# Diffusion steps on one core: tile 0's Sobel and first two steps moved forward, tile 1's coefficients behind them

## The chip, the cores and the metric

The kernel runs on 1 core of a Trainium2 chip: TensorE (PE), VectorE (DVE), ScalarE (ACT), GpSimd (POOL) and SyncE (SP) with a shared SBUF, PSUM in four slots of 1024 columns for this kernel, and 16 DMA engines. The time is the device time of one execution in microseconds; the median of 3 runs is compared.

## The reference, cut to what matters

The input is x of 8 x 32 x 32 x 64. A group norm gives s. A depthwise 3x3 convolution gives g and g1, Sobel gives the diffusivities, and five explicit steps of an advection and diffusion scheme follow. Its result is added to x, and a second part adds a ternary 3x3 convolution.

```python
gy, gx = _sobel(h)
Dx = 1.0 / (gy * gy / LAM2 + 1.0)
Dy = 1.0 / (gx * gx / LAM2 + 1.0)
ux = 0.5 * (jnp.roll(g, 1, axis=2) - jnp.roll(g, -1, axis=2))
vy = 0.5 * (jnp.roll(g1, 1, axis=3) - jnp.roll(g1, -1, axis=3))
Ax, Ay = (g * DT, g1 * DT)
Bx, By = (Dx * DT, Dy * DT)
E = (ux + vy) * DT
D = 1.0 / (1.0 + 2.0 * Bx + 2.0 * By)
cm_x, cp_x = (-Ax + 2.0 * Bx, Ax + 2.0 * Bx)
cm_y, cp_y = (-Ay + 2.0 * By, Ay + 2.0 * By)
c0 = 1.0 - 2.0 * Bx - 2.0 * By
for _ in range(K):
    prev = h
    h = D * (c0 * h0 - 2.0 * E * h + cm_x * jnp.roll(h, 1, axis=2) + cp_x * jnp.roll(h, -1, axis=2)
             + cm_y * jnp.roll(h, 1, axis=3) + cp_y * jnp.roll(h, -1, axis=3))
    h = h + D * (2.0 * DT) * fsrc
    h0 = prev
...
x = x + _L0_conv_ref(_gn(x), ...)   # the part above, with its last norm and relu
x = x + _L1_conv_ref(_gn(x), ...)   # y = conv(x, alpha * ternary(W)), relu(y + b)
```

## The kernel before

The batch is cut into two tiles of four images. A tile lies in SBUF with 128 partitions (image row and image) and planes of 2048 float32 columns (W x C); "a plane" below is one such 128 x 2048 block. `coef` holds seven planes of coefficients for each tile: AXP, AXM, AYP, AYM and AE multiply the four neighbours and the centre in a step, A0 the state before the last, and FS is the source. `ring` has three planes; early on they hold x, squares, regrouped s (`s_grouped`), g1 of tile 0 and `e0`, later the products.

The program is written per engine, in one fixed order, with semaphores between the engines. No scheduler moves anything. PSUM slots are given out by the table `early` in `job_table` and by the rows that the function adds from ORDER; TensorE takes a slot for a job (`take`) once the reader of the last job there has signalled (`wait_reader`).

The head of a tile, in its order: sums over the groups (`sum_x`, `centre`, `square_of`, `sum_squares`), small matmuls `mean_t` and `var_t`, rsqrt by Ln and Exp on ScalarE. Then `scale_grouped` (line 718) writes scaled s in another order of columns for the turns `t2`, and `scale_s` scales s in place. `split_hi` and `split_lo` cut s into two parts of reduced float32 for Sobel, which TensorE runs in passes over the high and the low part (`sobel`, line 1095): gy and gx, two halves each. ScalarE squares them into coef planes 0 and 1. `depthwise` (line 1123) makes g and g1 (PSUM jobs `cv_t_q`), which ScalarE reads with `to_natural`. VectorE's `shifted`, `denominator`, `newton`, `across_rows`, `across_columns`, `both_diffusivities` turn the squares into the coefficients, with one inverse by ScalarE's Ln and Exp (`reciprocal_first`), and `over_rows` and `over_channels` finish AXM, AXP, AYM and AYP of a tile.

GpSimd's queue carries DMAs that add one SBUF plane to another. For tile 0 the divergence e is made from VectorE's `channel_difference` (three instructions, the last signals `e_made`) and two pairs of adding DMAs (`e_some`, `e_full`), and `divergence_added` (line 873) turns it into AE. For tile 1 TensorE makes it (`divergence`, line 1145, two halves of two banks). Other adding DMAs are `other_rows` (AXM, semaphore `ax_full`), `other_channels` (AYM, `ay_full`), `first_source` (the plane `first_two` that TensorE adds in steps 0 and 1, `first_full`), the sum of tile 1's two diffusivities (`sb_added`, behind a copy by SP, `sb_begun`) and the kept plane of each later step.

A step (k, t) is `step` on VectorE (line 978): five products of a coefficient and the shifted state into the ring, and for k from 1 to 3 a sixth plane, the A0 product kept for the next step. TensorE adds each product into PSUM by 16 transposing matmuls (`add_products`), as well as the source or the kept plane (`add_source`), and turns the result back to natural order (`back_to_natural`) after ScalarE has copied it out (`keep_turned`, `keep_state`, `wrap` for the halo). VectorE can be at most three products ahead of TensorE. The steps of both tiles alternate by ORDER:

```python
ORDER = [(0, 0), (1, 0), (0, 1), (2, 0), (1, 1), (3, 0), (2, 1), (4, 0), (3, 1), (4, 1)]
```

Behind the steps stand the residual, the second group norm (`spread`, `second_norm`, `normalise`), the dense convolution as `dense` with high and low parts, and the way back (`out_natural`).

## Time and profile before

| | us |
|---|---|
| median of 3 runs (278.44 to 280.2) | 278.44 |
| the profiled execution, its own time | 277.91 |
| its span, first to last instruction | 276.1 |
| VectorE busy | 247.2 (90%) |
| TensorE busy | 233.6 (85%) |
| ScalarE busy | 133.8 (48%) |

The profile is of one execution. A line of the order of time gives the start, the time from the first start to the last end of the group, the engine, the line of the kernel, what it writes and reads, how many instructions there are, and in brackets the idle time of the engine ahead of it with what ended it. ScalarE's calls all carry line 380, a helper's, and VectorE's fused ones line 653; they are told apart by their tiles and times. Matmul ends are modelled; the distance between starts is the better measure.

### The profile page before, as it was taken

How to read it: one execution, taken by the hardware profiler on the slowest of the kernel's cores; microseconds unless marked ns; L12 is line 12 of the kernel's file. 1: busy time of each engine (PE TensorE's matmuls, PEld its weight loads, DVE VectorE, ACT ScalarE, POOL GpSimd, SP SyncE). 2: the span in 40 equal slices, each digit the busy share in tenths (PEclk: the TensorE clock that was granted, in tenths of full speed). 3: DMA queues.
4: the chain of work that ended last, by engine and by line, in shares of the span. 5: the costliest groups of instructions: out<-in, count | busy, mean ns of one | idle time of the engine just before them, and what ended most of it. 6: DMA issues, size and time to landing. Idle time of an engine off the chain costs nothing.

```text
span 276.1 us, 5235 instructions
## 1 busy us (share of the span) xinstructions
PE 233.6 (85%) x2276; PEld 209.6 (76%) x2276; DVE 247.2 (90%) x196; ACT 133.8 (48%) x207; POOL 16.8 (6%) x36
## 2 busy tenths in 40 slices
PE   0137999999959999279999999999999987889793
PEld 0136889989925588279989999898989986767683
DVE  3799999999999989999998999999999989886821
ACT  3294776879860054702623425160603246917743
POOL 2000000003310201101000101010101000000000
PEclk9999999999979999959999999999999999999999
DMA  6950000005998771990700334248610030000124
GB/s 213 350 116 0 0 4 6 2 0 112 199 205 253 152 152 38 209 209 2 154 0 2 76 78 94 61 116 190 129 26 1 0 138 17 2 0 0 62 93 152
DMA packets 7190, 24.94 MB, mean 90 GB/s; under 512 B 2816, under 2 KB 3328, under 8 KB 5120
## 3 DMA queue, kind: packets, MB, share of 16 engines
q0 software_dynamic: 2304, 14.68, 26.6%
q1 hardware_dynamic: 4720, 9.61, 10.6%
q10 hardware_dynamic: 144, 0.33, 0.4%
q8 instruction: 18, 0.29, 0.4%
q14 instruction: 4, 0.03, 0.0%
HBM read 6.79 MB, written 2.10 MB: 32 GB/s over the span
## 4 chain that ended last, share of the span: by engine, by line
DVE 54%; PE 27%; issue 9%; ACT 7%; DMA 1%; DVEq 0%; ACTq 0%
DVE ring L918 24%; DVE coef L653 8%; PE psum L1180 8%; PE psum L1170 6%; ACT coef L380 5%; PE psum L1257 5%; DVE first_two L1004 4%; PE psum L1117 3%; PE psum L1087 3%; DVE state L729 2%; DVE coef L964 1%; DMA bn<-in_norms 1%; DVE ring L722 1%; DVE hi_s L734 1%; DVE gsum L687 1%
## 5 line engine op out<-in xcount | busy, mean ns | idle before, releaser
L918 DVE TENSOR_TENSOR ring<-coef,state 128x2048 f32<-128x2048 f32 x51 | 113.5, 2286 | 2.1 <-PE psum L1180 1.9
L1180 PE MATMUL psum<-mats,ring 128*128 128x128 f32 x816 | 96.6, 278 | 9.6 <-DVE ring L918 9.5
L1180 PEld LDWEIGHTS psum<-mats,ring 128*128 128x128 f32 x816 | 91.4, 144 | 13.3 <-DVE ring L918 12.9
L380 ACT ACTIVATE state<-psum 128x1024 f32<-128x1024 f32 x36 | 35.1, 1028 | 74.3 <-PE psum L1180 60.2
L653 DVE SCALAR_TENSOR_TENSOR coef<-coef 128x2048 f32<-128x2048 f32 x16 | 36.4, 2290 | 0.7 <-issue 0.2
L380 ACT ACTIVATE coef<-coef 128x2048 f32<-128x2048 f32 (+1 forms) x10 | 17.6, 1783 | 10.1 <-DMA coef<-coef 9.9
L1257 PE MATMUL psum<-hi,dense_m 128*128 128x512 f32 (+1 forms) x54 | 20.0, 379 | 0.9 <-ACT coef L380 0.9
L1139 PEld LDWEIGHTS psum<-coef,state 32*128 32x128 f32 x672 | 19.4, 187 | 1.4 <-issue 1.3
L380 ACT ACTIVATE coef<-psum 128x512 f32<-128x512 f32 (+2 forms) x23 | 17.5, 766 | 5.4 <-PE psum L1117 4.3
L1139 PE MATMUL psum<-coef,state 32*128 32x64 f32 x672 | 20.0, 271 | 0.0
L1257 PE MATMUL psum<-lo,dense_m 128*128 128x512 f32 (+1 forms) x54 | 19.5, 369 | 0.0
L1180 PE MATMUL psum<-mats,first_two 128*128 128x128 f32 x144 | 17.3, 273 | 1.8 <-issue 1.2
L1180 PEld LDWEIGHTS psum<-mats,first_two 128*128 128x128 f32 x144 | 15.9, 141 | 2.3 <-ACT state L380 1.4
L1087 PE MATMUL psum<-mats,state 128*128 128x128 f32 x128 | 15.4, 273 | 0.7 <-ACT state L380 0.7
L1087 PEld LDWEIGHTS psum<-mats,state 128*128 128x128 f32 x128 | 14.1, 141 | 1.2 <-ACT state L380 1.1
L380 ACT ACTIVATE coef<-coef,gn 64x512 f32<-64x512 f32 x9 | 11.3, 1322 | 3.4 <-DVE gn L653 3.4
L975 DVE TENSOR_TENSOR coef<-coef 128x512 f32<-128x512 f32 (+2 forms) x7 | 5.4, 767 | 8.2 <-ACT coef L380 8.1
L1117 PE MATMUL psum<-hi_s,sobel_m 128*128 128x512 f32 (+2 forms) x48 | 12.1, 391 | 0.2 <-DVE hi_s L734 0.2
L1170 PE MATMUL psum<-coef,mats 128*128 128x512 f32 (+2 forms) x20 | 9.6, 616 | 3.1 <-ACT first_two L380 3.1
L1257 PEld LDWEIGHTS psum<-hi,dense_m 128*128 128x128 f32 x54 | 10.2, 188 | 2.7 <-issue 1.1
L380 ACT ACTIVATE coef<-psum,outp,wred 128x512 f32<-128x512 f32 (+2 forms) x7 | 5.9, 838 | 13.0 <-PE psum L1257 13.0
L1270 PE MATMUL psum<-gsum,mats 128*128 128x32 f32 x4 | 1.2, 404 | 12.2 <-DVE gsum L687 12.2
(133 smaller groups left out, 280.4 us busy)
## 6 DMA issues: line engine op xcount, KB each, us to landing
first_two<-coef POOLq DMA_DIRECT2D x7, 1024.0 KB, 8.5
coef<-coef POOLq DMA_DIRECT2D x5, 1024.0 KB, 8.8
coef<-in_x SPq DMA_DIRECT2D x2, 1024.0 KB, 6.0
coef<-in_wide_taps SPq DMA_DIRECT2D x3, 384.0 KB, 7.6
ring<-in_x SPq DMA_DIRECT2D x2, 512.0 KB, 6.0
ring<-in_x SPq DMA_DIRECT2D x1, 1024.0 KB, 10.3
coef<-coef SPq DMA_DIRECT2D x1, 1024.0 KB, 7.6
out<-coef SPq DMA_DIRECT2D x2, 512.0 KB, 3.1
```

The lines of the kernel that those rows point to most:

```text
L380: return nc.scalar.activation(dst, src, func, **kw)
L653: return V.scalar_tensor_tensor(out=out_ap, in0=in0, scalar=scalar, in1=in1, op0=op0, op1=op1)
L729: signal(V.tensor_tensor(s, s, root(t).unsqueeze(1).broadcast_to([128, W, C]), ALU.mult), s_ready, t + 1)
L918: V.tensor_tensor(wc(ring[:, slot, :]), wc(coef[:, t, a, :]), h_at(t, k, dw, dc), ALU.mult)\
L975: V.tensor_tensor(part(coef[:, t, 3, :], t, h), part(coef[:, t, 0, :], t, h), part(coef[:, t, 2, :], t, h), ALU.add).then_inc(sum_ready, 1)
L1004: V.tensor_tensor(wc(first_two[t][:, :]), wc(coef[:, t, A0, :]), h_at(t, k), ALU.mult)\
L1087: ins = nc.tensor.transpose(dst[:, j * 128:j * 128 + 128], src, ident)
L1117: ins = mm(dst[:, bank * BANK + to * C:bank * BANK + (to + count) * C], sobel_m[:, m, :], part[:, frm * C:(frm + count) * C], start=(i == ...
L1139: ins = mm(banks[a][:, j * 2 * W:(j + 1) * 2 * W], sT[t][p, 8 * h + j, dy * BT:dy * BT + 128], taps(8 * h + j)[p, dy, :, :].rearrange("p v ...
L1170: ins = mm(out_ap, m, src, start=(i == 0), stop=(i == len(pieces) - 1), skip_group_check=True)
L1180: ins = mm(slot_ap(name)[:, (j % 8) * 128:(j % 8) * 128 + 128], src[:, j * 128:j * 128 + 128], ident, is_transpose=True, start=first and j ...
L1257: ins = mm(to, dense_m[:, b, dy, :], rows[:, j0 + b:j1 + b, dy * BT:dy * BT + 128], start=(n == 0), stop=(n == len(steps) - 1))
```

## The change

The kernel does the same arithmetic with other orders and other homes for some work.

- VectorE scales s first and reorders it by a plain copy (`reorder`). Tile 0's high part and tile 1's reorder go to ScalarE.
- TensorE runs 12, 5 and 8 matmuls on `sobel_m` whose results nobody reads (`keep_warm`) between the small ones. Sobel of tile 0 comes ahead of its turns `t2`, gy's two high passes ahead of its low ones; tile 1's Sobel comes behind tile 1's depthwise and has SBUF of its own for its two parts.
- The divergence of tile 1 moves on TensorE from ahead of all steps to two places: a half after step (0, 0), a half after step (1, 0).
- VectorE runs tile 0's source and step (0, 0) ahead of tile 1's newton, with AE, `denominator(1)` and a small request between the products, and step (1, 0) ahead of tile 1's `over_rows`.
- GpSimd's queue runs both pairs of e first, then AXM, AYM and first_two of tile 0, then the rest.
- ScalarE's order for tile 1 follows. The last rsqrt stands ahead of `relu_dense(0, 0)`.
- `both_diffusivities`, `d_of(0)` and the first of `over_rows(0)` run in halves. The ring is used in falling order.

```diff
 (VectorE)
-            scale_grouped(0)
+            scale_s(0)
+            reorder(0)
             mean_of(1)
...
             threshold()
-            scale_s(0)
-            split_hi(0)
             split_lo(0)
             centre(1)
             sum_squares(1)
...
-            ternary()
+            ternary_count()
             ask_scale(1)
-            ternary_sign()
+            ternary_kept()
             rsqrt(128, GROUPS, root(1), wide=True)
-            scale_grouped(1)
+            scale_s(1)
             shifted(0)
             denominator(0)
-            scale_s(1)
+            weight_scale()
+            ternary_sign()
             split_hi(1)
             split_lo(1)
             newton(0)
             across_columns(0)
+            channel_difference()
             across_rows(0)
             both_diffusivities(0)
-            channel_difference()
             over_rows(0)
...
-            denominator(1)
             over_channels(0)
+            source(0)
+            step(0, 0, ((1, divergence_added), (2, lambda: denominator(1)), (3, ask_out)))
             newton(1)
+            out_norm()
             across_rows(1)
             across_columns(1)
-            divergence_added()
...
-            step(0, 0)
+            step(1, 0)
             over_rows(1)
             over_channels(1)
             divergence_taken()
             source(1)
-            step(1, 0)
 (VectorE's reorder)
+                dve.wait_ge(s_ready, t + 1)
+                V.tensor_copy(s_grouped[t].rearrange("p (g a w e) -> p a w g e", e=2, a=CP, w=W),
+                              h_at(t, 0).rearrange("p w (a g e) -> p a w g e", a=CP, e=2)).then_inc(s_grouped_ready, 1)
 (GpSimd)
-            other_rows(0)
             pool.wait_ge(e_some, 32)
             pool.wait_ge(minus_ready, 1)
             pool.dma_start(e0[:, 0:N - C], minus_g[:, C:N], accum_op=ALU.add).then_inc(e_full, 16)
             pool.dma_start(e0[:, N - C:N], minus_g[:, 0:C], accum_op=ALU.add).then_inc(e_full, 16)
+            pool.wait_ge(e_full, 32)
+            other_rows(0)
             other_channels(0)
+            first_source(0)
             pool.wait_ge(sb_begun, 16)
 (TensorE)
+            def keep_warm(name, count):
+
+                to = take(name)[:, 0:BANK]
+                pe.wait_ge(sobel_m_ready, 4)
+                for _ in range(count):
+                    mm(to, sobel_m[:, 0, :], sobel_m[:, :, :].rearrange("p m n -> p (m n)"), start=True, stop=True)
+
             group_mean(0)
+            keep_warm("gx_0_0", 12)
             group_var(0)
+            keep_warm("gx_0_0", 5)
             group_mean(1)
...
             small("wsum", 1, ones[:, :], wred[:, 0:1])
-            to_depthwise(0, 0)
-            to_depthwise(0, 1)
-            pe.wait_ge(sobel_m_ready, 4)
-            sobel(0, 0, 0)
-            sobel(0, 0, 1)
+            keep_warm("gx_0_0", 8)
+            for n in range(2):
+                sobel(0, 0, 0, (n,))
+                sobel(0, 0, 1, (n,))
...
-            divergence(0)
-            divergence(1)
+            for g in range(2):
+                for h in range(2):
+                    sobel(1, g, h)
             last = None
             for k, t in ORDER:
-                if last is None:
-                    take_sums(t, k)
-                    add_products(t, k, ((2, lambda: add_source(*reversed(ORDER[0]), False)),), True)
-                    last = (k, t)
-                    continue
-                if last[0] < STEPS - 1 and last[1] == t:
+                if last is not None and last[0] < STEPS - 1 and last[1] == t:
+                    back_to_natural(*last)
+                if (k, t) == ORDER[1]:
+                    divergence(0)
+                if (k, t) == ORDER[2]:
+                    divergence(1)
                     back_to_natural(*last)
                 if (k, t) == ORDER[-1]:
                     group_mean2(0)
                 take_sums(t, k)
+                if k == 0:
+                    add_products(t, k, ((3, lambda: add_source(t, 0, False)),), True)
+                    last = (k, t)
+                    continue
                 add_source(t, k)
 (ScalarE, the last norm)
             relu_bn_out(1, 0)
             relu_bn_out(1, 1)
+            rsqrt_first(128, BT)
             relu_dense(0, 0)
-            rsqrt_first(128, BT)
             normalise(1)
```

On GpSimd's queue, behind the first pair of e, the program before has this order (`coef<-coef` at line 316 is AXM, 321 is AYM, 340 the sum of tile 1's diffusivities, 335 and 336 the second pair of e):

```order
L330 DMA ring<-coef 128x1984 [waits e_made]
L331 DMA ring<-coef 128x64
L316 DMA coef<-coef 128x2048 [waits axp_ready]
L335 DMA ring<-state 128x1984 [waits minus_ready,e_some]
L336 DMA ring<-state 128x64
L321 DMA coef<-coef 128x2048 [waits ayp_ready]
L340 DMA coef<-coef 128x2048 [waits column_part,sb_begun]
L327 DMA first_two0<-coef 128x2048 [waits s_copied0,source_ready]
```

The changed program has the same queue in this order (326 is AXM, 331 AYM, 352 the sum, 344 and 345 the second pair):

```order
L340 DMA ring<-coef0 128x1984 [waits e_made]
L341 DMA ring<-coef0 128x64
L344 DMA ring<-state 128x1984 [waits minus_ready,e_some]
L345 DMA ring<-state 128x64
L326 DMA coef0<-coef0 128x2048 [waits axp_ready,e_full]
L331 DMA coef0<-coef0 128x2048 [waits ayp_ready]
L337 DMA first_two0<-state 128x2048 [waits s_copied0,source_ready]
L352 DMA coef1<-coef1 128x2048 [waits column_part,sb_begun]
```

AXM moved behind the end of e, and tile 0's first_two moved in front of tile 1's sum.

On VectorE, the changed program has this around step (0, 0); `ring<-coef0,state` is a product, 917 is AE, the lines 683 on coef1 are `denominator(1)` and `newton(1)`:

```order
L683 SCALAR_TENSOR_TENSOR state<-coef0,state 128x2048 [waits pe_job]
L960 TENSOR_TENSOR ring<-coef0,state 128x2048 [waits pe_job,axp_ready,ayp_ready,s_halo]
L960 TENSOR_TENSOR ring<-coef0,state 128x2048 [waits dense_m_ready]
L917 TENSOR_TENSOR coef0<-ring,coef0 128x2048 [waits e_full,d_ready,axp_ready]
L960 TENSOR_TENSOR ring<-coef0,state 128x2048 [waits ae_ready]
L683 SCALAR_TENSOR_TENSOR coef1<-coef1 128x2048 [waits shifted_ready,slot_free1,slot_free0]
L960 TENSOR_TENSOR ring<-coef0,state 128x2048 [waits ring_free,ax_full0,u_ready]
L1060 TENSOR_SCALAR rs_in<-outp 128x1 [waits outp_in]
L960 TENSOR_TENSOR ring<-coef0,state 128x2048 [waits ring_free,ay_full0,rs_asked]
L683 SCALAR_TENSOR_TENSOR coef1<-coef1 128x2048 [waits y_ready]
```

Before, all of `denominator(1)`, `newton(1)`, the two across planes and AE stood ahead of the first product; now the first two products stand ahead of AE and the rest of tile 1 stands between or behind.

On TensorE, the changed program has this from the fourth product of step (0, 0) on (1229 adds a plane by 16 transposes, 1134 turns back, 1219 is the divergence):

```order
L1229 MATMUL psum<-mats,ring 128x128 x15
L1229 MATMUL psum<-mats,first_two0 128x128 [waits first_full0]
L1229 MATMUL psum<-mats,first_two0 128x128 x15
L1229 MATMUL psum<-mats,ring 128x128 [waits product]
L1229 MATMUL psum<-mats,ring 128x128 x15
L1134 MATMUL psum<-mats,state 128x128 [waits slot_free0]
L1134 MATMUL psum<-mats,state 128x128 x7
L1134 MATMUL psum<-mats,state 128x128 [waits slot_free1]
L1134 MATMUL psum<-mats,state 128x128 x7
L1219 MATMUL psum<-coef1,mats 128x512 [waits slot_free2,slot_free3,slot_free1,slot_free0]
```

Before, the source came behind the third product, and both halves of the divergence ahead of the first.

## Rows read from the trace of the kernel before

**Rows 1.** The page, part 1: busy time, share of the span, instructions.

```profile
PE 233.6 (85%) x2276; PEld 209.6 (76%) x2276; DVE 247.2 (90%) x196; ACT 133.8 (48%) x207; POOL 16.8 (6%) x36
```

**Rows 2.** VectorE's order of time, head; columns as told under the profile.

```profile
19.87 2.29 DVE L722 TENSOR_TENSOR ring<-state,gsum 128x2048 f32<-128x2048 f32 x1
...
24.75 1.23 DVE L734 CAST hi_s<-state 128x2048 fp32r<-128x2048 f32 x1
...
35.55 0.19 DVE L714 TENSOR_SCALAR rs_in<-psum 128x32 f32<-128x32 f32 x1 [0.37 <-PE psum L1276]
```

**Rows 3.** ScalarE's order of time: copy_s(0), d_of(1) with a0_of(1), wrap of state 1.

```profile
78.77 1.97 ACT L380 ACTIVATE first_two<-state 128x2048 f32<-128x2048 f32 x1
...
97.51 3.73 ACT L380 ACTIVATE coef<-coef 128x2048 f32<-128x2048 f32 x2 [9.93 <-DMA coef<-coef]
...
111.45 0.71 ACT L380 ACTIVATE state<-state 128x64 f32<-128x64 f32 x4
```

**Rows 4.** VectorE's order of time, from the end of channel_difference to step (2, 0).

```profile
63.36 0.21 DVE L871 TENSOR_TENSOR ring<-ring 128x32 f32<-128x32 f32 x1
...
98.49 4.49 DVE L918 TENSOR_TENSOR ring<-coef,state 128x2048 f32<-128x2048 f32 x2 [1.16 <-PE psum L1180]
102.90 4.61 DVE L653 SCALAR_TENSOR_TENSOR coef<-coef 128x2048 f32<-128x2048 f32 x2
...
129.84 11.10 DVE L918 TENSOR_TENSOR ring<-coef,state 128x2048 f32<-128x2048 f32 x5
...
148.23 4.50 DVE L918 TENSOR_TENSOR ring<-coef,state 128x2048 f32<-128x2048 f32 x2 [0.69 <-PE psum L1180]
```

**Rows 5.** TensorE's order of time: first Sobel passes, and tile 1's turns behind tile 0's depthwise.

```profile
26.12 2.50 PE L1117 MATMUL psum<-hi_s,sobel_m 128*128 128x512 f32 x7 [0.22 <-DVE hi_s L734]
28.45 1.65 PE L1117 MATMUL psum<-lo_s,sobel_m 128*128 128x512 f32 x7
...
50.43 2.19 PE L1087 MATMUL psum<-mats,ring 128*128 128x128 f32 x16
```

**Rows 6.** TensorE's order of time: divergence, step (0, 0) and step (2, 0).

```profile
84.76 1.96 PE L1170 MATMUL psum<-coef,mats 128*128 128x512 f32 x4
...
96.44 5.44 PE L1180 MATMUL psum<-mats,ring 128*128 128x128 f32 x48
102.52 1.97 PE L1180 MATMUL psum<-mats,first_two 128*128 128x128 f32 x16 [0.65 <-DMA first_two<-coef]
104.32 3.66 PE L1180 MATMUL psum<-mats,ring 128*128 128x128 f32 x32
108.32 1.98 PE L1087 MATMUL psum<-mats,state 128*128 128x128 f32 x16 [0.34 <-ACT state L380]
...
146.28 8.90 PE L1180 MATMUL psum<-mats,ring 128*128 128x128 f32 x80
```

**Rows 7.** GpSimd's and SP's order of time: DMA issues around e and tile 1's sum.

```profile
72.02 0.86 POOL L335 DMA_DIRECT2D ring<-state  x1 [2.51 <-DMA ring<-coef]
...
90.53 0.86 POOL L340 DMA_DIRECT2D coef<-coef  x1 [13.66 <-DMA coef<-coef]
...
82.67 0.51 SPq L289 DMA_DIRECT2D coef<-coef  x1
```

**Rows 8.** Stretches: us, TensorE busy, its granted clock, DMA share, GB/s.

```profile
79.20:84.70 5.50, 5.50 (x14) 0.71 1.06 205
...
92.00:97.00 5.00, 5.00 (x23) 1.00 0.99 198
...
118.00:121.00 3.00, 2.04 (x10) 0.50 1.09 216
```

**Rows 9.** The page, part 6: adding DMAs between planes of coef, median us to landing.

```profile
coef<-coef POOLq DMA_DIRECT2D x5, 1024.0 KB, 8.8
```

**Rows 10.** ScalarE's and VectorE's order of time: relu ahead of the last rsqrt.

```profile
249.70 1.21 ACT L380 ACTIVATE coef<-psum,outp,wred 128x1024 f32<-128x1024 f32 x1 [7.01 <-PE psum L1257]
...
251.27 0.16 DVE L670 TENSOR_TENSOR rs_t<-rs_y 128x4 f32<-128x4 f32 x1 [1.91 <-ACT rs_y L380]
```

285 lines of the change are left out of this document (159 added, 126 removed), and 6 rows, old and new, of the table early.

## Prediction

> **What bounds the kernel now.** The page's busy line [rows 1] shows VectorE busy for 247.2 of 276.1 us and TensorE for 233.6. VectorE's order of time [rows 2, 4] shows that it hardly waits between the first mean and 98 us. Each step of the recurrence then costs it six full planes at 2.2 us, 13.2 us; TensorE needs seven passes of 16 transposes at 1.75 us, 12.3 us (80 took 8.90 in [rows 6]). So TensorE has 0.9 us to spare in a step, and only after a step without a sixth plane (k = 0) does it make VectorE wait: 1.16 us at 98.49 and 0.69 us at 148.23 [rows 4]. I read the change at two places: where VectorE ends tile 0's first step together with tile 1's inverse (102.98 before), and where it makes the fourth product of step (2, 0) (148.23 before). From there to the last norm both programs are alike and VectorE does not wait.
>
> All times are on the axis of the profiled execution: its span is 276.1 us, its own time 277.91 us, and the median of the three runs 278.44. I sum changes of the span and take them from 278.44.
>
> **The head, up to e.** On VectorE the change removes two scale_grouped at 2.29 and one cast at 1.23, and adds one reorder of a full plane [rows 2]. The trace has no such copy; its bounds are the cast (1.23) and the strided scale_grouped (2.29). I take 1.23, the price of a one-source full plane here. Removed: 4.6 us (3.5 with the other bound). Waits come in return:
> - s is ready at 19.87 + 2.29 = 22.2. ScalarE's high part is a full plane out of state, 1.97 as in copy_s [rows 3]: 24.2, where the cast ended at 25.98. VectorE is there at 23.8 and waits 0.4.
> - The warm-up matmuls stand between the sums: 12 of 512 columns from about 11.6. Seven at the slow start took 2.50 us [rows 5], 0.36 each, twice the full rate would be 0.43, so 12 end at 15.9 to 16.8; var_0's sums are ready at 16.65. Cost 0 to 0.15, taken as 0. If they work, the first Sobel pass takes 1.65 and not 2.50.
> - TensorE: four passes of 1.5 us from 24.3, then gx_0_0 (2.1), then var_1 at 32.5. VectorE waits 0.4 for it, as it does now (0.37 in [rows 2]). Sobel ends at 35.1, the turns of tile 0 at 37.0, and after ScalarE's copy and alpha the depthwise of tile 0 runs from 37.3, 13.1 us. It ends at 50.4, as before [rows 5]: this side gains nothing.
> - ScalarE: squares to 36.1, two copies to 38.1, four taps to 39.2, reorder(1) as a full plane to 41.2, Ln and Exp of tile 0 to 45.2. VectorE is through denominator, alpha, sign and tile 1's parts at 46.2: hidden by 1.0. Were reorder(1) 2 us slower, 1 us would show.
> - channel_difference now stands ahead of across_rows and needs cv_0_3 read. ScalarE reads cv_0_2 from 50.5 (1.0), then copies half of t2_1 (1.0), then reads cv_0_3 (1.0): 53.6. VectorE is there at 53.1 and waits 0.5.
>
> So e is made at 56.2 instead of 63.57 [rows 4]; across_rows, the two halves of both_diffusivities, the first over_rows (in halves as well, behind d_of's halves of 1.0), over_channels and source, seven planes of 2.3, end at 72.4.
>
> **Tile 0's first step.** Two products (76.8), AE (79.1), its product (81.3), denominator(1) (83.7; shifted(1) is done at 79.1, since TensorE's Sobel of tile 1 runs from 65.8 to 75.9), product (85.9), product (88.3). Newton(1) needs ScalarE's Ln and Exp of the denominator: 87.7, hidden. With newton 4.6, the output norm 1.2 and two across planes 4.6 VectorE is at 98.7. Before, the same list ended at 102.98: gain 4.3, of which 1.16 is the old wait at 98.49, and 4.6 removed less 0.9 of new waits and some halves make the rest.
>
> **The adding DMAs, which become the bound.** The queue works in order and moves 198 GB/s while it adds [rows 8], so 1 MB takes 5.3 us after 1.5 us of start: the one issued at 90.53 was waited for until 97.51, the next until 102.52 [rows 3, 6, 7]. From e made to the second pair went 63.57 to 72.02, 8.45 us [rows 4, 7]. So the first pair runs 56.2 to 64.65, and the second, now alone on the queue, 0.8 + 7.0 more: 72.5. Then three adds follow together, 1.5 + 3 x 5.3: AXM 79.4, AYM 84.8, first_two0 90.1. AXM and AYM are needed at 83.7 and 86.1: hidden by 4.3 and 1.3. first_two0 is not: TensorE has added the fourth product by 87.8 and must add the source before the fifth. Its order is then source 91.9, fifth product 93.7, turns back to natural 96.0 (2.3 later, as 107.98 to 110.30 in [rows 6]), half the divergence at 3.9 per bank (three banks from 84.76 to 96.44): 103.8. Then source of (1, 0) 105.6, first product 107.3. The halo of state 1 comes 4.2 after the fifth product (107.98 to 112.16 in [rows 3, 6]): 97.9, just hidden by VectorE's 98.7.
>
> VectorE makes three products of (1, 0) by 105.3 and then finds the ring full until 107.4: a new wait of 2.1. Two products and the kept plane: 114.0. Tile 1's d is ready at 96.4 + 7.9 (SP's copy, 82.67 to 90.53 in [rows 7]) + 7.0 (add) + 2.1 = 113.4, hidden by 0.6. Tile 1's rows, channels, divergence and source are six planes, 13.8: step (0, 1) starts at 127.8, before at 129.84. Gain left 2.0.
>
> **Step (0, 1).** Its source moves from the front to place 3, in front of the fifth product. TensorE ends the fourth at 138.5 and the fifth at 142.0; then source and turns of (2, 0) and one product, 5.3 more: VectorE's fourth product of (2, 0) starts 19.6 after the step's start, before 18.4 (129.84 to 148.23). Minus 1.2. Further, TensorE has nothing from 125.5 to 130.1. After such a gap the granted clock was 0.50 (the 1.2 GHz level) in 118 to 121 [rows 8], so its first passes run slow: 0 to 1.0, I take 0.6. So 148.23 becomes 148.0: **gain 0.2 of the 4.3**.
>
> **The tail.** The last rsqrt moves in front of relu_dense(0, 0). ScalarE stood idle when it was asked, but ran 1.21 us of relu first; VectorE waited 1.91 [rows 10]. VectorE is free 1.5 earlier, ScalarE's three pieces 1.05, TensorE's dense(1, 0), which follows the low half, 1.3. From there it is TensorE's work to the end: **minus 1.3**.
>
> Sum: 0.2 + 1.3 = 1.5, 278.44 - 1.5 = **276.9 us**.
>
> **A rule weighed.** From 92 to 97 us the adds moved 198 GB/s [rows 8]. The Trainium skill, DMA: Bandwidth & Descriptors, section Measured (HBM→SBUF), gives 6.15 us and 341 GB/s for one transfer of 1 MB issued from GpSimd. By that rate three adds would take an estimated 9.2 us of transfer instead of 16, first_two0 would be there near 83, and the sum would be that of rival 2. That table is for plain loads, and this trace disagrees with it for adds within SBUF.
>
> **The rivals.**
> 1. The clock falls in tile 0's first step. TensorE works there in pieces, with gaps of 2.0, 2.7 and 2.2 us from 79 to 90. For: after an idle stretch of 3 us it averaged 0.71 in 79.2 to 84.7 [rows 8]. Against: shorter gaps left it at 1.00. A slow pass costs 1.75 more, and one to two are on the path of first_two0: 1.7 to 3.5, 279.3. It decides over the sum from any fall at 90.
> 2. VectorE stays the bound: e or the adds are earlier and first_two0 lands before 88, so the 2.1 wait goes, and with it the 0.6: 274.2. For: the 1.5 of start is read from one pair only. Against: 198 GB/s.
> 3. Slower: the adds don't overlap their fixed parts, and each lands 8.8 us after the last (the median of five in [rows 9]). first_two0 lands at 98.9, 8.8 later, and all to 148 with it: 285.7. It makes the kernel slower by 1% once first_two0 lands after 94.5. Against it: the pair at 90.53.
> 4. The warm-up does nothing: the first high pass stays 0.85 longer, and var_1 with it: 277.7. Against it: TensorE runs at full rate from 28.45 [rows 5], after some 6 us of work, and would have had that work before.
>
> **How the numbers follow.** The likeliest, the sum as worked out, 0.45 (its own range 275.0 to 278.8: reorder 0 to 1.1, slow start 0 to 1.0, one microsecond either way for the head); rival 1 0.19; rival 2 0.22; rival 3 0.06; rival 4 0.08. Range 273.8 to 280.0, from rival 2 to the middle of rival 1. One percent, 2.8 us, is about what a measurement of this kernel can tell. Faster by more: rival 2 and a fifth of the likeliest, 0.31. Slower by more (over 281.2): rival 3 and the upper end of rival 1, 0.11. The rest 0.58.
>
> **What would show it.** The high part on ScalarE ends near 24.2; e is made near 56; three adds are issued together at 72 to 73; TensorE waits for the DMA of first_two0 until 90, with the clock beside it; VectorE waits some 2 us for TensorE in the fourth product of (1, 0), and again in that of (2, 0); step (0, 1) starts near 127.8; the wait for the last rsqrt is 0.4 instead of 1.91. The prediction is wrong if VectorE doesn't wait in (1, 0), if first_two0 lands away from 90, or if ScalarE's strided reorder costs far more than 2 us.

## Result: 0.7% slower

| | changed kernel | kernel before |
|---|---|---|
| median of 20 runs each | 280.76 us (278.16 to 283.38) | 278.56 us (277.73 to 280.2) |
| ratio, 95% interval | 1.0069 (1.0052 to 1.0086) | 1 |
| profiled execution: own time, span | 283.38, 281.6 us | 277.91, 276.1 us |
| VectorE, TensorE busy | 243.5, 242.6 us | 247.2, 233.6 us |
| mean granted clock of TensorE | 0.964 | 0.981 |

The forecast was 276.9 us, with a range to 280.0. The profiled execution of the changed kernel is the longest of its twenty, 2.6 us over the median, and one of three slow ones that the ratio leaves out; its late times exceed those of a median run by up to as much. Experiments are compared by their ratios, and a difference between two of them carries the intervals of both. The page, part 1, of the changed kernel (it answers [rows 1]):

```profile
PE 242.6 (86%) x2301; PEld 216.9 (77%) x2301; DVE 243.5 (86%) x196; ACT 138.2 (49%) x210; POOL 16.9 (6%) x36
```

VectorE does 3.7 us less, as the change intends, and the kernel is still slower. The time went into waits. VectorE's order of time, changed kernel, those waits (it answers [rows 2, 4]):

```profile
34.62 0.19 DVE L744 TENSOR_SCALAR rs_in<-psum 128x32 f32<-128x32 f32 x1 [2.05 <-PE psum L1325]
...
55.84 2.23 DVE L908 TENSOR_TENSOR ring<-ring 128x1984 f32<-128x1984 f32 x1 [1.18 <-ACT ring L391]
...
85.20 2.29 DVE L683 SCALAR_TENSOR_TENSOR coef<-coef 128x2048 f32<-128x2048 f32 x1 [1.84 <-ACT coef L391]
...
103.98 6.70 DVE L960 TENSOR_TENSOR ring<-coef,state 128x2048 f32<-128x2048 f32 x3 [1.55 <-ACT state L391]
113.39 2.29 DVE L960 TENSOR_TENSOR ring<-coef,state 128x2048 f32<-128x2048 f32 x1 [2.71 <-PE psum L1229]
...
133.71 8.89 DVE L960 TENSOR_TENSOR ring<-coef,state 128x2048 f32<-128x2048 f32 x4
...
154.92 4.50 DVE L960 TENSOR_TENSOR ring<-coef,state 128x2048 f32<-128x2048 f32 x2 [2.94 <-PE psum L1229]
```

In order: var_1 from TensorE 2.05 (0.37 before); channel_difference 1.18; tile 1's shifted magnitudes at denominator(1) 1.84; the halo of state 1 1.55; the full ring in (1, 0) 2.71; the fourth product of (2, 0) 2.94 (0.69 before, at 148.23). TensorE's order of time, changed kernel, shows what they wait for (it answers [rows 5, 6]):

```profile
20.12 2.08 PE L1332 MATMUL psum<-sobel_m 128*128 128x512 f32 x8
24.38 4.50 PE L1165 MATMUL psum<-hi_s,sobel_m 128*128 128x512 f32 x14 [2.17 <-ACT hi_s L391]
...
62.66 4.01 PE L1188 MATMUL psum<-coef,state 32*128 32x64 f32 x133
68.38 0.55 PE L1188 MATMUL psum<-coef,state 32*128 32x64 f32 x10 [1.71 <-issue]
...
94.64 3.38 PE L1229 MATMUL psum<-mats,first_two 128*128 128x128 f32 x16 [1.89 <-DMA first_two<-state]
...
136.14 10.01 PE L1229 MATMUL psum<-mats,ring 128*128 128x128 f32 x64 [6.28 <-DVE ring L960]
```

Each stall is followed by slow work. Stretches of the changed kernel (length, TensorE busy, then its weight loads and the other engines; the granted clock is third from the right, then DMA share and GB/s):

```profile
26.00:28.00 2.00, 2.00 (x6) 1.62 (x5) 2.00 (x3) 1.10 (x5) 0.00 (x0) 0.50 0.00 0
...
70.00:72.00 2.00, 2.00 (x16) 1.70 (x13) 2.00 (x1) 1.78 (x4) 0.00 (x0) 0.57 1.28 254
...
92.00:94.00 2.00, 0.75 (x4) 0.35 (x2) 2.00 (x2) 0.00 (x0) 0.00 (x0) 0.50 0.37 74
...
136.00:142.00 6.00, 5.86 (x28) 5.89 (x29) 6.00 (x3) 0.00 (x0) 0.00 (x0) 0.50 0.98 198
```

0.50 is the 1.2 GHz level. The pause of 1.71 us at 66.67 has no releaser in the trace ("issue") and no counterpart before.

### The profile page after: what moved, and what is told of

It is laid out like the page before. It is cut to its first block, busy times and chain, and to the rows that moved or that the text cites. A ratio compares the mean times of both kernels' runs of the same rounds, so it can differ in the third digit from the quotient of the medians.

```text
span 281.6 us, 5289 instructions
## 1 busy us (share of the span) xinstructions
PE 242.6 (86%) x2301; PEld 216.9 (77%) x2301; DVE 243.5 (86%) x196; ACT 138.2 (49%) x210; POOL 16.9 (6%) x36
## 4 chain that ended last, share of the span: by engine, by line
DVE 28%; PE 20%; issue 3%; ACT 1%; DVEq 0%; ACTq 0%
DVE ring L960 19%; PE psum L1229 12%; PE psum L1306 4%; DVE first_two L1046 3%; PE psum L1134 3%; DVE coef L1006 2%; DVE coef L968 1%; DVE stats L973 1%; DVE coef L1017 1%; DVE lo L1012 0%; DVE coef L925 0%; ACT state L391 0%; ACT coef L391 0%; DVE gn L683 0%; PE psum L1285 0%
## 5 line engine op out<-in xcount | busy, mean ns | idle before, releaser
L1229 PE MATMUL psum<-mats,ring 128*128 128x128 f32 x816 | 98.2, 280 | 12.7 <-DVE ring L960 12.6
L1229 PEld LDWEIGHTS psum<-mats,ring 128*128 128x128 f32 x816 | 92.8, 145 | 16.1 <-DVE ring L960 9.2
L683 DVE SCALAR_TENSOR_TENSOR coef<-coef 128x2048 f32<-128x2048 f32 (+1 forms) x17 | 36.6, 2164 | 2.3 <-ACT coef L391 1.8
L391 ACT ACTIVATE coef<-coef 128x2048 f32<-128x2048 f32 (+2 forms) x10 | 16.0, 1614 | 10.2 <-DMA coef<-coef 7.1
L1229 PE MATMUL psum<-mats,first_two 128*128 128x128 f32 x144 | 18.7, 287 | 1.9 <-DMA first_two<-state 1.9
L1229 PEld LDWEIGHTS psum<-mats,first_two 128*128 128x128 f32 x144 | 17.4, 150 | 2.3 <-DMA first_two<-state 2.3
L1165 PE MATMUL psum<-hi_s,sobel_m 128*128 128x512 f32 (+2 forms) x48 | 13.9, 438 | 2.2 <-ACT hi_s L391 2.2
L1165 PEld LDWEIGHTS psum<-hi_s,sobel_m 128*128 128x128 f32 x48 | 10.2, 227 | 4.5 <-issue 2.6
L1306 PEld LDWEIGHTS psum<-hi,dense_m 128*128 128x128 f32 x54 | 10.1, 188 | 3.0 <-issue 1.1
L1165 PE MATMUL psum<-lo_s,sobel_m 128*128 128x512 f32 (+2 forms) x48 | 11.6, 383 | 0.0
L1046 DVE TENSOR_TENSOR first_two<-coef,state 128x2048 f32<-128x2048 f32 x5 | 11.4, 2289 | 0.0
```

The costliest lines, as they stand in the source:

```text
L391: return nc.scalar.activation(dst, src, func, **kw)
L683: return V.scalar_tensor_tensor(out=out_ap, in0=in0, scalar=scalar, in1=in1, op0=op0, op1=op1)
L1046: V.tensor_tensor(wc(first_two[t][:, :]), wc(coef[t][:, A0, :]), h_at(t, k), ALU.mult)\
L1165: ins = mm(dst[:, bank * BANK + to * C:bank * BANK + (to + count) * C], sobel_m[:, m, :], part[:, frm * C:(frm + count) * C], start=(i == ...
L1229: ins = mm(slot_ap(name)[:, (j % 8) * 128:(j % 8) * 128 + 128], src[:, j * 128:j * 128 + 128], ident, is_transpose=True, start=first and j ...
L1306: ins = mm(to, dense_m[:, b, dy, :], rows[:, j0 + b:j1 + b, dy * BT:dy * BT + 128], start=(n == 0), stop=(n == len(steps) - 1))
```

## Experiments

Each ratio is to the kernel before. "Unread matmuls" are matmuls whose result nobody reads. Three theories compete. **Clock**: TensorE's granted clock falls after each gap. **Chain of adds**: tile 0's source lands too late. **Sobel(1) late**: tile 1's Sobel now stands behind depthwise(1), and VectorE needs it in the middle of step (0, 0).

**tail_only**: the kernel before, with the last rsqrt ahead of relu_dense(0, 0).

```diff
-            relu_dense(0, 0)
             rsqrt_first(128, BT)
+            relu_dense(0, 0)
             normalise(1)
```

> The kernel before with one edit of the change: the last rsqrt ahead of relu_dense(0, 0). All theories expect VectorE's wait there to fall from 1.91 to 0.4 us and the end to come 1.2 to 1.3 us earlier: 277.3 us, ratio 0.9955. If it stays at 1.00 the tail's gain is lost again in the dense part.

277.38 us, 0.9962 (0.9946 to 0.9978): 1.06 us gained of 1.3 forecast. VectorE's wait of 1.91 [rows 10] became 0.38. So the other parts of the change together cost 1.07 points, some 3.0 us.

**fill_gaps**: the changed kernel with unread matmuls in TensorE's gaps.

```diff
-            keep_warm("gx_0_0", 8)
+            keep_warm("gx_0_0", 18)
...
+                    keep_warm("acc_0_1_0", 22)
...
+                    if (k, t) == ORDER[0]:
+                        between = ((2, lambda: keep_warm("dv_1_0", 8)), (3, lambda: keep_warm("dv_1_0", 9))) + between
```

> The changed kernel with matmuls nobody reads in three gaps of TensorE: 18 instead of 8 ahead of Sobel, 8 and 9 behind the third and fourth product of step (0, 0), 22 ahead of step (0, 1). The clock theory (slow passes after gaps: 24.4, 70, 91 and 136 us in the profile of the changed kernel) expects 2 to 4 us back: 277 to 279 us, and a narrower spread of runs, since the fall depends on the run. The theory of the adding DMAs (first_two0 is what binds, the slow passes are mostly hidden) expects at most 1 us: 280 us.

281.41 us (280.96 to 281.93), 1.011 (1.0093 to 1.0128). The mean clock rose from 0.964 to 0.986 and e was made 2.0 us earlier (56.3), yet the kernel is 1.1 us slower than the changed one. VectorE's wait at denominator(1) grew to 3.52. The clock alone is not the cause. In step (2, 0) TensorE waited 1.62 us for the kept plane's add, a wait that I had not seen coming.

**div_gap**: divergence(0) between the third and the fourth product of (0, 0), into TensorE's gap of 2.6 us.

```diff
-        if i == 1:
+        if i == 0:
             jobs.append(("dv_1_0", 2))
...
-                if (k, t) == ORDER[1]:
-                    divergence(0)
...
+                    if (k, t) == ORDER[0]:
+                        between = ((2, lambda: divergence(0)),) + between
```

> The changed kernel with the first half of tile 1's divergence moved on TensorE from behind step (0, 0) to between its third and fourth product, where TensorE has nothing to do. The theory that the divergence stands on the path of VectorE's ring expects the wait of 2.71 us in step (1, 0) to vanish, and the slow source pass with it: 3 to 4 us, 277 to 278 us. If the adds alone bind, the halo of state 1 stays where it is and only the ring wait goes: 278 us. The clock theory without the path expects 1 us: 279.7.

280.61 us, 1.0085 (1.0054 to 1.0116): no gain. The full ring's wait of 2.71 us is gone, but the halo's wait rose to 2.07 and the one at denominator(1) was 3.44.

**no_ewait**: GpSimd no longer waits for the second pair before it issues tile 0's adds.

```diff
-            pool.wait_ge(e_full, 32)
             other_rows(0)
```

> The changed kernel without GpSimd's wait for e between the second pair and AXM (the add of AXM touches nothing of e). The theory that the chain of adds binds expects AXM's transfer to start right behind e's, 3 to 4.5 us earlier, first_two0 as much earlier, and 2 to 3 us off the time: 278 us. Against it: AXM's transfer may hold up the end of e's pair, then AE is late and the time stays at 280.5. The clock theory alone expects at most 1 us.

279.92 us, 1.0045 (1.002 to 1.007): 0.7 us under the changed kernel, which is less than the two intervals together. AXM, AYM and the source are issued at 67.5, 72.0 and 74.2 instead of 76.2 to 77.3, and TensorE no longer waits for the source; VectorE waits 3.44 at denominator(1) instead. Whether the adds are part of it is open until queue_both.

**den_late**: denominator(1) behind the fifth product.

```diff
+            rsqrt_first(128, 1)
             reciprocal_first(1)
-            rsqrt_first(128, 1)
...
-            step(0, 0, ((1, divergence_added), (2, lambda: denominator(1)), (3, ask_out)))
-            newton(1)
+            step(0, 0, ((1, divergence_added), (3, ask_out), (4, lambda: denominator(1))))
             out_norm()
+            newton(1)
```

> The changed kernel with denominator(1) behind the fifth product of step (0,0), so that VectorE no longer waits in the middle of that step for the shifted magnitudes of tile 1. Theory 'Sobel(1) is late' (wait of 1.84 us in the profile of the changed kernel, 3.44 us in two variants of it): the five products of step (0,0) end 1.5 to 3.4 us earlier, and of that 1 to 2 us reach the end, 278.5 to 280 us; newton(1) may then wait for ScalarE's Ln and Exp. Theory 'TensorE's clock': the wait is only moved, and the time stays at 280.5 to 281.5 us. Theory 'the chain of adds': the ready adds still land at their time, so the halo wait in front of step (1,0) grows by what was gained, 280 to 281 us.

282.45 us, 1.0129 (1.0095 to 1.0162): slower than the changed kernel by 1.7 us. VectorE's order of time, den_late, and the issue of AYM's add at 76.25 with its time to landing:

```profile
83.33 2.29 DVE L960 TENSOR_TENSOR ring<-coef,state 128x2048 f32<-128x2048 f32 x1 [0.52 <-PE psum L1229]
...
89.27 2.29 DVE L960 TENSOR_TENSOR ring<-coef,state 128x2048 f32<-128x2048 f32 x1 [3.58 <-issue]
...
97.85 9.22 DVE L683 SCALAR_TENSOR_TENSOR coef<-coef 128x2048 f32<-128x2048 f32 x4 [2.92 <-ACT coef L391]
```

```profile
coef<-coef POOLq DMA_DIRECT2D x1, 1024.0 KB, 12.9
```

With denominator(1) out of the way the fourth product waits 0.52 us itself, for TensorE: it starts to add products only when Sobel(1) ends, at 81.3, and the ring has three planes. The fifth waits 3.58, and not for TensorE: it needs AYM, whose add was issued at 76.25 and landed 12.9 us later, at 89.2, and the product starts at 89.27. In the changed kernel AYM landed at 89.70 and the fifth product started at 89.91: it was hidden by 0.2 us, behind the wait at denominator(1). So two bounds lie close together here, Sobel(1) and the adds. newton(1) then waits 2.92 us for ScalarE's inverse, which now starts later, and step (1, 0) begins at 107.0 and not at 104.0.

**sobel_fill**: 18 instead of 8 unread matmuls ahead of Sobel(0), the first line of fill_gaps alone.

> The changed kernel with 18 instead of 8 unread matmuls between Sobel(0)'s coefficients being asked for and its first pass; nothing else. Theory 'TensorE's clock': the 14 high-pass matmuls of Sobel(0) take 3.0 instead of 4.5 us, VectorE's wait for var_1 (2.05 us) falls under 0.5, the gain of tile 0 is made by 56.3 instead of 58.3, and the time falls by 1.5 to 2 us to about 279 us. Theory 'what comes behind': the earlier gain is eaten by waits for Sobel(1) and the adds, and the time is within 0.7 us of the changed kernel's.

279.51 us, 1.0038 (1.0015 to 1.0062): 0.9 us gained on the changed kernel. The wait for var_1 fell to 0.44, the first pair was issued 1.6 us earlier, and the wait at denominator(1) grew to 4.31. TensorE's order of time and stretches, sobel_fill:

```profile
66.53 1.33 PE L1188 MATMUL psum<-coef,state 32*128 32x64 f32 x19 [1.69 <-issue]
```

```profile
66.00:68.00 2.00, 1.47 (x28) 1.47 (x32) 2.00 (x2) 1.93 (x7) 1.46 (x2) 0.50 0.12 24
68.00:70.00 2.00, 2.00 (x46) 2.00 (x43) 1.97 (x2) 0.04 (x1) 0.29 (x1) 0.50 1.18 230
70.00:72.00 2.00, 2.00 (x14) 1.65 (x14) 1.93 (x2) 1.55 (x4) 0.00 (x0) 0.50 0.93 190
72.00:74.00 2.00, 2.00 (x7) 1.61 (x6) 2.00 (x2) 0.52 (x2) 0.00 (x0) 0.50 0.55 87
```

The pause is there again, ten matmuls earlier in depthwise(1, 1) with ten more in front of it: behind the 850th matmul since the start, as in the changed kernel. Behind it the clock is at 0.50 until 74. That eats the gain: Sobel(1) ends at 82.9, in the changed kernel at 81.8.

**kept_first**: GpSimd's add of (2, 0)'s kept plane ahead of tile 1's whole-tile adds.

```diff
+            keep(1, 0)
             other_rows(1)
...
-            for k, t in ORDER:
+            for k, t in ORDER[2:]:
```

> The changed kernel with GpSimd's add of the kept plane for step (2,0) put ahead of tile 1's whole-tile adds. Theory 'the kept plane is late' : step (2,0)'s fourth product no longer waits 2.9 us for TensorE, and up to 1.3 us comes off, 279.5 us. Theory 'TensorE's clock' : the stall of TensorE ahead of step (0,1) stays, (2,0) stays as late, and the time is within 0.5 us of the changed kernel's. The add now stands ahead of tile 1's adds in the queue and could hold them for 5.3 us: then step (0,1) starts later and the time rises by 1 to 3 us.

280.2 us, 1.0049 (1.0025 to 1.0073), 0.2 points under the changed kernel, less than the two intervals together. VectorE's wait in (2, 0) was 2.10.

**no_warm**: the three keep_warm counts at 0.

> The changed kernel without its 25 unread matmuls (counts 12, 5 and 8 set to nothing). Theory 'TensorE's clock': the box sums and Sobel(0) run at the lower clock, var_0 and var_1 come 1 to 3 us later, the gain of tile 0 is made at 60 to 61 and the time rises by 2 to 3 us to about 283 us. Theory 'the warm-up warms nothing that matters': within 0.7 us of the changed kernel. TensorE's unexplained pause of 1.7 us in depthwise(1,1) stays at its place among the instructions if it is tied to the program, and goes if it is tied to what TensorE did before.

283.96 us, 1.0184 (1.0159 to 1.0209): the warm-up is worth 3.2 us, a little over the 2 to 3 that I expected. The pause shrank to 0.93 us. It stands later in depthwise(1, 1) but again behind some 850 matmuls, since 25 are missing in front.

**sobel_early**: TensorE's Sobel(1) and ScalarE's squares ahead of depthwise(1), with the PSUM slots to match; of the edit TensorE's part:

```diff
...
-            depthwise(1, 0)
-            depthwise(1, 1)
             for g in range(2):
                 for h in range(2):
                     sobel(1, g, h)
+            depthwise(1, 0)
+            depthwise(1, 1)
```

> The changed kernel with TensorE's Sobel of tile 1 ahead of the depthwise sums of tile 1, as the kernel before had it; ScalarE's squares go with it, and nothing else changes. Theory 'the order depthwise, then Sobel, is the harm': TensorE's pause of 1.7 us in the depthwise sums of tile 1 and the half clock behind it no longer stand ahead of the shifted magnitudes, VectorE's wait at denominator(1) goes (1.84 to 4.3 us so far), and the products of step (0,0) end 2 to 3 us earlier. What reaches the end is bounded by the adds, since the source of tile 0 is needed ahead of the fifth product and lands near 94 us as before: 1 us, 279.5 to 280. Theory 'TensorE has the same work to do and is the bound from 24 to 88 us': the wait only moves to the products, and the time is within 0.5 us of the changed kernel's.

285.98 us, 1.0257 (1.0227 to 1.0286), a miss that both theories share: source(0) writes the buffer out of which depthwise(1) reads, and VectorE waited 9.37 us for it. The change's order of the two is forced by that buffer. The pause was there all the same (1.11 us, the clock at 0.50 in 77 to 79), again behind the 848th matmul, although these now include all 48 of Sobel(1). So it belongs to a count of TensorE's instructions and not to Sobel's place.

**best2** is no_ewait, sobel_fill and kept_first together; **best3** adds sobel_early to it, **best4** div_gap to best3.

> The three single edits without sobel_early: no wait for the second e pair ahead of tile 0's adds, 18 unread matmuls ahead of Sobel(0), the kept plane's add ahead of tile 1's. Alone they were worth 0.8, 0.9 and 0.5 us. Theory 'each cures its own delay': 278.3 to 278.8 us. Theory 'the wait for the shifted magnitudes of tile 1 is what they all run into': it grows to 4 us or more and the time stays at 279.3 to 280 us; the difference to best3 is then what the order of Sobel and depthwise costs.

> sobel_early together with the three single edits that gained: no wait for the second e pair ahead of tile 0's adds, 18 instead of 8 unread matmuls ahead of Sobel(0), and the kept plane's add ahead of tile 1's. If the parts add up, 0.9 + 0.8 + 0.5 and what sobel_early is worth: 277.5 to 278.5 us, even with the kernel before or just ahead of it. If one bound takes over from the next, as the wait for shifted(1) did when the others were taken away, 279 to 280 us.

> best3 with the first half of tile 1's divergence between the third and fourth product of step (0,0), where TensorE waits for VectorE. With the source of tile 0 landed in time, the half divergence (3.9 us) is off the path from the fifth product to the first sum of step (1,0), and the full ring in (1,0) (1.6 us in the profile without the wait for the e pair) goes: up to 1.5 us under best3 if that wait is the bound there; within 0.5 us of best3 if VectorE only waits later, in step (2,0).

best2: 278.95 us, 1.0014 (0.9993 to 1.0034), level with the kernel before; the parts nearly add up (0.24 + 0.31 + 0.20 points expected, 0.55 measured). best3: 286.14 us, 1.0234; best4: 286.74 us, 1.0283; both carry sobel_early's wait and tell no more. In best2 TensorE still waits 6.28 us ahead of (0, 1), then takes 9.93 us for 64 transposes, and the pause is there.

**no_e_adds**: the changed kernel without the four adding DMAs into e and the waits for them. This leaves out two of e's terms; it measures only what they cost.

```diff
-            pool.dma_start(e0[:, C:N], gN[0][:, 0:N - C], accum_op=ALU.add).then_inc(e_some, 16)
...
-            pool.dma_start(e0[:, N - C:N], minus_g[:, 0:C], accum_op=ALU.add).then_inc(e_full, 16)
```

> The changed kernel without the two pairs of adding DMAs into e and without the waits for them; this leaves out part of the computation of e, and its time is only for comparison. The adds of tile 0 are then issued from 67.5 us, and the queue is empty while TensorE runs the first part of the depthwise sums of tile 1. Theory 'the adds' transfers hold up TensorE's load of instructions': the pause of 1.7 us in the depthwise sums of tile 1 goes, the clock stays at 1.00 from 66 to 76, Sobel(1) ends near 79 instead of 81.8, and VectorE's wait at denominator(1) is 0 to 1.5 us instead of 1.84 to 3.4. Theory 'the pause belongs to the program': it stays at its place with 1.5 to 1.8 us. In both cases the source of tile 0 lands by 88 us, so TensorE doesn't wait for it: with the pause gone 277.5 to 278.5 us, with it 279 to 279.8.

276.43 us, 0.992 (0.9896 to 0.9944): 4.1 us under the changed kernel. TensorE's order of time and two stretches, no_e_adds:

```profile
63.02 4.25 PE L1179 MATMUL psum<-coef,state 32*128 32x64 f32 x144
67.09 1.52 PE L1179 MATMUL psum<-last_taps,state 32*128 32x64 f32 x48
68.54 1.74 PE L1156 MATMUL psum<-hi_s,sobel_m 128*128 128x512 f32 x7
```

```profile
66.00:68.00 2.00, 2.00 (x83) 2.00 (x79) 2.00 (x2) 2.00 (x6) 0.00 (x0) 1.00 0.03 8
...
70.00:72.00 2.00, 2.00 (x11) 1.69 (x10) 1.97 (x2) 1.98 (x6) 0.00 (x0) 1.00 1.10 221
```

No pause, full clock, Sobel(1) over at 78.5, and no wait at denominator(1) or for the halo. Without the adds into e there is no pause. The three later adds are also earlier here: the source lands at 87.1 and not at 94.6.

**best5** is best2 with 22 unread matmuls ahead of step (0, 1); **best6** adds div_gap.

> best2 with 22 unread matmuls of 512 columns ahead of step (0, 1), where TensorE stood idle for 6.28 us and then ran 64 transposes in 9.93 us. Theory 'the clock there feeds the wait of step (2, 0)': TensorE runs that step at 1.00, VectorE's wait of 2.95 us at the fourth product of (2, 0) falls to 1.2 or less, and the time is 277.0 to 277.8 us. Theory 'TensorE is short of time in the steps of five products whatever the clock': the wait stays over 2 us and the time within 0.5 us of best2.

> best5 with the first half of tile 1's divergence between the third and fourth product of step (0, 0). It takes TensorE's idle stretch of 2.6 us there, and the wait for the full ring in (1, 0) (1.58 us in best2) goes. Theory 'each cures its own delay': 0.8 to 1.5 us under best5. Theory 'half a divergence is 3.9 us and the gap only 2.6': the fifth product of step (0, 0) and the halo behind it come 1 to 2 us later, VectorE waits there instead, and best6 is within 0.5 us of best5.

best5: 278.24 us, 0.9982 (0.9964 to 0.9999), 0.9 us under best2. The wait in (2, 0) fell from 2.95 to 1.99 and no further; about a microsecond of it was the clock. best6: 279.69 us, 1.0037: the halo is late by 2.08 in place of the full ring, the second reading that I gave.

**split_e**: the large add of the first pair in four pieces. **best7**: the same on top of best5.

```diff
-            pool.dma_start(e0[:, C:N], gN[0][:, 0:N - C], accum_op=ALU.add).then_inc(e_some, 16)
+            for a, b in ((C, 512), (512, 1024), (1024, 1536), (1536, N)):
+                pool.dma_start(e0[:, a:b], gN[0][:, a - C:b - C], accum_op=ALU.add).then_inc(e_some, 16)
...
-            pool.wait_ge(e_some, 32)
+            pool.wait_ge(e_some, 80)
```

> The changed kernel with the large add of the first pair into e cut into four adds of up to 512 columns; the same bytes and sums. Theory 'a load of instructions waits behind long transfers': TensorE's pause of 1.7 us falls under 0.8 us or goes, the clock behind it stays higher, and VectorE's wait for tile 1's shifted magnitudes shrinks; but three more issues at 0.7 us on GpSimd and shorter pieces make the pair 0 to 3 us longer, so the time is 279 to 281 us. Theory 'any adds at that time do it': the pause stays and the time is 280.5 to 282 us.

> best5 with the same cut of the first pair. If the pause goes, 276.5 to 277.8 us, at or under the kernel before with the tail alone (277.4); if it stays, 278 to 279.5 us.

The pause is gone in both, and the clock is 1.00 from 60 to 80 us. best7: **275.7 us** (275.54 to 276.69), 0.9917 (0.9896 to 0.9937), 0.45 points under tail_only and the best of all. split_e alone: 281.52 us, 1.0115 (1.0093 to 1.0136), 1.3 us slower than the changed kernel. TensorE's order of time, split_e: the source is late as ever, and slow behind it:

```profile
91.68 3.36 PE L1230 MATMUL psum<-mats,first_two 128*128 128x128 f32 x16 [3.73 <-DMA first_two<-state]
```

The DMA queues show how the pause arises. Queue 8 loads instructions, 18 times 16 KB (the page counts 0.29 MB); with 4602 matmuls and weight loads that is one load per 256 of them, so by this estimate the loads are TensorE's. The queue's row for 65.75 to 66.00 us of the changed kernel:

```profile
q8 instruction: 1, 0.02, 23.4%
```

The load before that one started at 58.42. The table has the load that the pause hangs on, from the packets of each trace; "landed" is the large add into e, or its second piece.

| | landed | load starts | matmuls by then | pause behind | length | ends after the load's start |
|---|---|---|---|---|---|---|
| best3 | 71.76 | 71.80 | 843 | 848 | 2.02 | 2.48 |
| best5 | 63.57 | 63.75 | 839 | 850 | 1.68 | 2.31 |
| changed kernel | 65.64 | 65.94 | 833 | 850 | 1.71 | 2.44 |
| sobel_early | 72.80 | 73.08 | 817 | 848 | 1.11 | 2.28 |
| no_warm | 65.66 | 65.95 | 810 | 849 | 0.93 | 2.31 |
| kernel before | 70.93 | 71.20 | 776 | no pause | | |
| queue_both | 63.26 | 63.67 | 765 | no pause | | |
| best7 | 61.53 | 61.64 | 763 | no pause | | |
| split_e | 61.63 | 61.79 | 757 | no pause | | |
| no_e_adds | no add | 62.91 | 717 | no pause | | |

In all fourteen traces with a pause (the changed kernel and thirteen variants) it stands behind the 848th to 850th matmul, it ends 2.2 to 2.5 us after the load has started, and the load starts 0.04 to 0.31 us after a 992 KB add into e has landed (of the second pair in sobel_early, best3 and best4). So the place is fixed by the number of instructions, and the length by how few matmuls lie between the load and that place. Where the load starts 85 matmuls or more ahead of it, there is no pause. In the kernel before the add delays the load too, but only 776 matmuls have been issued by then; its 850th is issued at 73.41, 2.2 us after the load. If its place is the same, which no run shows, the load was just in time.

The Trainium skill, Runtime: NRT & Kernel Launch, section Instruction fetch mechanics, says that an engine refills its instructions in blocks of 16 KiB over a DMA queue of its own and calls the cost "mostly hidden". The size agrees with this trace; hidden the load was only where it started early enough. The Trainium skill, DMA: Bandwidth & Descriptors, section Queues, rings and completion order, lets each DMA engine change between queues at the end of a packet. The trace agrees with this only in part. In the changed kernel the large add is 128 packets of 7936 bytes of some 0.63 us, eight for each DMA engine, and the load starts behind the last of them; in split_e it starts behind the second of four pieces. When the load was asked for no trace shows; if that was before the add's end, it waited for a whole transfer and not for one packet.

**queue_both**: the changed kernel with no_ewait and split_e and nothing else.

> The changed kernel with only the two edits to GpSimd's queue: the first pair into e cut into five transfers, and no wait for the second pair ahead of tile 0's adds. Alone they gave 281.5 and 279.9 us (changed kernel 280.8). Theory 'the two hide each other': without the pause there is no wait for tile 1's shifted magnitudes, without the wait for the pair TensorE finds the source of tile 0 landed, and VectorE no longer waits for the halo in front of step (1, 0): 277.3 to 278.5 us. Theory 'the edits simply add': 280.5 us. Theory 'best7 owes its time to the unread matmuls': 279.5 us or more.

278.78 us, 1.0002 (0.9978 to 1.0026), 1.9 us under the changed kernel, where the two alone gave -0.7 and +1.3. Together they give 2.5 us more than their sum, with an interval of 1.2 either way. VectorE's order of time, queue_both:

```profile
101.29 6.70 DVE L960 TENSOR_TENSOR ring<-coef,state 128x2048 f32<-128x2048 f32 x3 [1.15 <-ACT state L391]
110.70 4.50 DVE L960 TENSOR_TENSOR ring<-coef,state 128x2048 f32<-128x2048 f32 x2 [2.71 <-PE psum L1229]
...
151.48 4.50 DVE L960 TENSOR_TENSOR ring<-coef,state 128x2048 f32<-128x2048 f32 x2 [2.76 <-PE psum L1229]
```

The two hide each other. With the pause alone cured, TensorE waits longer for the source; with the source alone early, VectorE waits longer for Sobel(1). Without the pause the earlier adds are worth 3.1 us (queue_both against split_e), with it 0.7, not clear of noise.

## Why the prediction was wrong

| step | predicted | changed kernel |
|---|---|---|
| reorder copy on VectorE; on ScalarE | 1.23; 2.0 | 1.30; 2.07 |
| high part on ScalarE ends | 24.2 | 24.24 |
| first pass of Sobel(0), 14 matmuls | 3.0 | 4.50 |
| VectorE waits for var_1 | 0.4 | 2.05 |
| e made | 56.2 | 58.3 |
| second pair into e | 7.8 | 9.5 |
| three adds issued | 72.5 | 76.2 to 77.3 |
| Sobel(1) | 65.8 to 75.9 | 70.3 to 81.8 |
| tile 0's source there | 90.1 | 94.6 |
| first product of (1, 0) | 98.7 | 103.98 |
| full ring in (1, 0) | 2.1 | 2.71 |
| step (0, 1) starts | 127.8 | 133.7 |
| fourth product of (2, 0), after that start | 20.2 | 21.2 |
| the tail | -1.3 | -1.06 (tail_only) |

**Where the time went.** In the changed kernel's trace the adds are what ends last in tile 0's first step: VectorE was through its own list at 102.4 (forecast 98.7, late through var_1 and denominator(1)) and then waited 1.55 us for the halo, which follows from the source's landing and its slow pass. That makes 5.3 us at the first product of (1, 0). Up to the start of (0, 1) 0.6 more are added, up to the fourth product of (2, 0) 1.0 more: 6.9 us against the forecast. The profiled execution is 2.6 us over the median; what is left is near the 3.9 us by which the median misses the forecast.

**Right**: VectorE's and ScalarE's durations, the tail, the full ring in (1, 0), that the adds bound tile 0's first step, and that the steps give back much of what the head gains. The last shows in best7, where both delays are cured: its source lands at 89.3 (forecast 90.1) and its first product of (1, 0) starts at 98.35 (98.7), 4.6 us ahead of the kernel before; at the fourth product of (2, 0), at 146.88, 1.35 us are left. The prediction itself said that the kernel gets slower by 1% once the source lands after 94.5; it landed at 94.6, and the kernel is 0.7% slower.

**Wrong: "If they work, the first Sobel pass takes 1.65 and not 2.50."** They worked: the last eight took 2.08 us, 0.26 each, the fast rate. But between them and Sobel(0) TensorE stood idle for 2.17 us, which my own times contain (24.3 against the end of the eight), and the clock fell to 0.50 in 26 to 28. The price of 0.36 each at the start was applied, the gap behind the warm-up was not looked at. Worth 1.65 us in the wait for var_1, and 0.9 us at the end by sobel_fill. The fall is not certain: of the nine traces with 8 matmuls and this gap eight show it between 24 and 28 us, and split_e's does not, with a wait for var_1 of 0.44. With 18 matmuls up to the work no trace shows it. Rival 4, which had this wait, argued that the warm-up does nothing; no_warm says 3.2 us.

**Wrong: denominator(1) without a wait, "since TensorE's Sobel of tile 1 runs from 65.8 to 75.9".** It had 2.2 us to spare (shifted(1) at 79.1, needed at 81.3). Sobel(1) began 4.5 us late: 1.9 for Sobel(0) and the turns (depthwise started at 39.2 and not at 37.3), 1.7 for the pause, 0.9 for small waits. It then took 11.5 us and not 10.1, at a clock of 0.57 to 0.58 in 70 to 74. I costed the transfers of e by their own length and by what waits for them, not by what they do to TensorE's load of instructions while depthwise(1) runs. Taking them away gave back 4.1 us, as much as the whole miss of 3.9; since tile 0's source is also there earlier without them, that is the pause and the chain together. Curing both and leaving the adds in gave back 1.9 us (queue_both).

**Wrong in size: the adds.** They land 4.5 us later than forecast, 2.1 from e, 1.7 from the second pair and the rest from the three adds themselves. Rival 1, the clock in tile 0's first step, came in on top as it was described: 0.50 in 92 to 94, 3.38 us for the source's pass. It was priced at 279.3 alone. Cases that I had listed as rivals occurred together, and the range, which ended in the middle of rival 1, did not allow for that.

**Missing: the kept plane of (2, 0)**, queued behind tile 1's adds. It shows as 1.62 us of TensorE's time once the clock is kept up (fill_gaps); kept_first, 0.2 points, doesn't settle its worth.

**A rule weighed.** The estimate of 9.2 us for three adds went by the rate in the row that it took from the Trainium skill, DMA: Bandwidth & Descriptors, section Measured (HBM→SBUF). The same row gives 6.15 us for 1 MB, which is 170 GB/s and would make 18.5 us by this estimate. The changed kernel's three adds took 18.4 us from the first issue to the last landing, so the trace agrees with the row's time and not with its rate. The sum used neither.

**Open.** Why split_e alone has a higher median than the changed kernel. Its trace doesn't show it: it is the fastest of its six executions (280.55) beside the slowest of twenty (283.38), 2.0 of its 3.1 us of advantage come from the clock ahead of Sobel(0), where the two programs are alike, and from e made to the first product of (1, 0) it is 1.0 us shorter. That the adds hold back the load, and the late load TensorE, is read from times that repeat in all the traces; no run moved the load alone.

## What to carry to other kernels

A large transfer can cost time on an engine that neither reads nor writes its data: look in the trace for idle time with no releaser on the engine with the most instructions, see whether it stays behind the same number of them from variant to variant and whether a load of instructions has just begun, and cut the transfer in front of that load into pieces. When two delays meet in one place, curing one alone may show nothing or a loss, so try the pair before dropping either. Unread matmuls that warm TensorE must reach up to the work they are meant for.

## What was not expected of the hardware

- An add of 992 KB into e, issued as one transfer, held back a 16 KB load of instructions: it started 7.5 us behind the one before and not 4.0, within 0.31 us of the add's landing, and TensorE paused for 0.9 to 2.0 us with nothing to wait for, each time behind the 848th to 850th matmul. With the add in four transfers of up to 512 columns the loads lay 5.3 to 5.8 us apart, without a pause.
- After that pause the granted clock was 0.50 from 66 to 74 us in sobel_fill, with TensorE busy nearly throughout; after the idle 2.17 us ahead of Sobel(0) it was 0.50 in 26 to 28 in the changed kernel and stayed at 1.00 in split_e's profiled execution.
- The time of one kernel's executions goes with this clock: best6 took 277.52 us at a mean of 0.994 and 281.42 at 0.976.
